# The causal attention product moved from the second slot of a step to the end of the first

## The reference, cut to what matters

```python
xn = layernorm(x)
# causal attention, 16 heads of 16
score = einsum('bhqd,bhkd->bhqk', Q, K) / sqrt(16) + mask
a = einsum('bhqk,bhkd->bhqd', softmax(score), V) @ WO
# attention with experts, 16 heads of 64, 8 experts, the best 2 of them
gv, go = gate(x, Wsel_v), gate(x, Wsel_o)
v   = einsum('bsd,bhse,hedp->bhsp', x, gv, Wv)
att = softmax(einsum('bhsp,bhtp->bhst', rope(x Wq), rope(x Wk)) / sqrt(64))
o   = einsum('bhst,bhtp->bhsp', att, v)
src = layernorm(x + einsum('bhsp,bhse,hepd->bsd', o, go, Wo))
y   = layernorm(src + relu(src @ W1 + b1) @ W2 + b2)
out = x + a + y
```

## Time and profile before

| what | value |
|---|---|
| time, median of 3 executions | 3246.9 us (3245.41 to 3250.37) |
| the profiled execution's own time | 3245.74 us |
| its span, first to last instruction | 3243.9 us |
| mean granted clock of TensorE | 0.991 of full speed |
| TensorE busy with matmuls | 3145.1 us, 97% |
| VectorE busy | 2480.0 us, 76% |
| ScalarE busy | 2017.9 us, 62% |
| GpSimd busy | 1477.1 us, 46% |

### The profile page before, as it was taken

The page is one execution under the profiler, slowest core; times in us unless marked ns, Lnnn a source line. Parts: engine busy times, 40 slices in busy tenths (PEclk is TensorE's granted clock), DMA queues, the critical chain, the costliest instruction groups (busy, mean ns, idle before and its releaser), DMA issues.

```text
span 3243.9 us, 67075 instructions
## 1 busy us (share of the span) xinstructions
PE 3145.1 (97%) x19648; PEld 2408.8 (74%) x19648; DVE 2480.0 (76%) x4686; ACT 2017.9 (62%) x4635; POOL 1477.1 (46%) x1231
## 2 busy tenths in 40 slices
PE   4899999999999999999999999999999999998997
PEld 3677777777777777777777777777777777775886
DVE  7777777777777778777787777777777777776896
ACT  4666666666666666666666666666666666664443
POOL 5233544335543444334543444434444543446677
PEclk8999999999999999999999999999999999999999
DMA  5232332333333332333323333243332433324222
GB/s 189 79 92 72 106 98 75 85 96 101 79 80 85 96 101 73 86 101 90 91 72 88 94 96 90 70 109 85 88 86 74 109 85 88 80 73 119 79 85 78
DMA packets 116202, 294.25 MB, mean 91 GB/s; under 512 B 33856, under 2 KB 54592, under 8 KB 99776
## 3 DMA queue, kind: packets, MB, share of 16 engines
q1 hardware_dynamic: 116160, 293.73, 33.9%
HBM read 261.69 MB, written 31.98 MB: 91 GB/s over the span
## 4 chain that ended last, share of the span: by engine, by line
PE 89%; DVE 7%; ACT 1%; POOL 1%; issue 1%; DMA 0%; SPq 0%; DVEq 0%; POOLq 0%; ACTq 0%
PE bank L753 32%; PE bank L896 22%; PE bank L811 11%; PE bank L768 7%; PE bank L869 6%; PE bank L773 2%; PE bank L881 2%; PE bank L1005 2%; PE bank L849 2%; PE bank L840 2%; PE bank L774 1%; PE bank L1016 1%; DVE nmax L1344 0%; DVE root L1262 0%; DVE rstd L1264 0%
## 5 line engine op out<-in xcount | busy, mean ns | idle before, releaser
L609 POOL TENSOR_TENSOR u_l<-uf,u_h 128x512 fp32r<-128x512 f32 x508 | 671.1, 1332 | 1624.3 <-ACT u_h L1177 1624.3
L753 PE MATMUL bank<-wv_h,xx 128*128 128x512 f32 x2048 | 735.7, 410 | 5.2 <-DVE vm L1362 5.2
L1087 ACT ACTIVATE probs<-bank,nmax 128x512 f32<-128x512 f32 (+3 forms) x1024 | 591.4, 606 | 234.2 <-DVE nmax L1344 229.9
L1344 DVE TENSOR_REDUCE nmax<-bank 128x1 f32<-128x512 f32 (+3 forms) x1024 | 554.2, 583 | 80.3 <-PE bank L774 52.8
L753 PEld LDWEIGHTS bank<-wv_h,xx 128*128 128x128 f32 x2048 | 386.9, 189 | 168.6 <-issue 80.4
L1177 ACT ACTIVATE u_h<-uf 128x512 fp32r<-128x512 f32 x508 | 304.9, 627 | 314.0 <-DVE uf L1449 314.0
L811 PEld LDWEIGHTS bank<-ident_sb,probs 128*128 128x128 f32 x3328 | 388.3, 141 | 106.9 <-issue 52.9
L811 PE MATMUL bank<-ident_sb,probs 128*128 128x128 f32 x3328 | 450.7, 274 | 0.9 <-ACT stackT L1162 0.9
L896 PE MATMUL bank<-u_h,wo_h 128*128 128x512 f32 x1016 | 430.3, 423 | 7.7 <-ACT q_h L1177 6.2
L1362 DVE TENSOR_TENSOR vm<-bank,gv 128x512 f32<-128x512 f32 x512 | 351.2, 686 | 81.6 <-PE bank L753 81.6
L896 PE MATMUL bank<-u_l,wo_h 128*128 128x512 f32 x1016 | 404.6, 398 | 0.0
(11 more groups left out here) (201 smaller groups left out, 5468.3 us busy)
## 6 DMA issues: line engine op xcount, KB each, us to landing
go<-go_d SPq DMA_DIRECT2D x256, 512.0 KB, 6.5
xx<-xs_d SPq DMA_DIRECT2D x126, 512.0 KB, 3.3
oo<-scale_d SPq DMA_DIRECT2D x128, 128.0 KB, 2.9
a_d<-a_out SPq DMA_DIRECT2D x128, 128.0 KB, 2.3
st<-in_wv SPq DMA_DIRECT2D x16, 512.0 KB, 5.6
st<-in_wo SPq DMA_DIRECT2D x16, 512.0 KB, 7.9
pt_c<-in_x SPq DMA_DIRECT2D x12, 512.0 KB, 4.8
go_d<-go_turned SPq DMA_DIRECT2D x256, 8.0 KB
```

What stands on the lines that cost most here:

```text
L609: nc.gpsimd.tensor_tensor(low, full, high.bitcast(f32), ALU.subtract).then_inc(ul_done, 1)
L753: last = nc.tensor.matmul(out, lhs, rhs, start=n == 1, stop=n == 3 * len(chunks))
L1087: nc.scalar.activation(probs[:, s % 2, j, 0:w], sbank[j][:, 0:w], ACT.Exp, bias=nmax[:, 2 * s + j:2 * s + j + 1], **kw).then_inc(exp_done, 1)
L1344: nc.vector.tensor_reduce(nmax[:, 2 * s + j:2 * s + j + 1], sbank[j][:, 0:w], AX.X, ALU.max, negate=True).then_inc(nmax_ready, 1)
```

## The change

In the table of TensorE's jobs, `AC` moves from the head of slot 1 to the end of slot 0. In an INNER step TensorE issued the scores of unit 1, `P` 0 to 3, `AT`, the transposes of unit 0, the scores of unit 2, `AC`, `V` 0, `V` 1. It now issues the scores of unit 1, `P` 0 to 3, `AT`, `AC`, the transposes of unit 0, the scores of unit 2, `V` 0, `V` 1. The tables of the other engines stay as they are. `AC` stays the sixth of the jobs that share the two banks, so the banks and the semaphore counts are the same.

```diff
-PE_FILL = [[("P", 0), ("P", 1), ("P", 2), ("P", 3), ("AT", 0)],
-           [("AC", 0), ("V", 0), ("V", 1), ("J", 0)],
+PE_FILL = [[("P", 0), ("P", 1), ("P", 2), ("P", 3), ("AT", 0), ("AC", 0)],
+           [("V", 0), ("V", 1), ("J", 0)],
            [("J", 1)],
            [("V", 2), ("J", 2), ("J", 3)],
```

## The result

| | before | after |
|---|---|---|
| median | 3247.1 us (3245.41 to 3251.13, 6 runs) | 3263.1 us (3261.7 to 3265.54, 6 runs) |
| span of the profiled execution | 3243.9 us | 3261.6 us |
| granted clock of TensorE, mean | 0.991 | 0.992 |

The ratio is 1.0049, with a 95% interval of 1.0038 to 1.0061: slower by half a per cent, 16 us. The forecast was 3264.

What follows compares the result with a forecast made beforehand. TensorE's issue time plus its few stalls was taken to bound the kernel. 55 usual steps × 0.33 us, less 0.7 in the seven late ones, made +17.5 us on 3245.7: 3263.2, as median 3264; range 3246 to 3287.

Steps and rivals of the forecast that it cites:

- The change of form: TensorE, AT and AC touching in 32-column pieces: V 0 comes 0.13 to 0.14 us earlier, 8.5 us over 63 steps.
- The maximum of unit 2: VectorE's row maximum, a sign: waits for TensorE's line 768 every step, starting 6.66 us behind AT, 0.92 late.
- ScalarE's copy stops waiting: Sign: the copy of a_out no longer waits for TensorE, so GpSimd's UL 1 starts about 7.3 us behind AT.
- Lines 1387, 1388 and 1390 are held: VectorE's CH 1, stretched by GpSimd instead of line 1404; U 2 comes 0.55 us late, the step grows by 0.33.
- The stall: TensorE's scores of unit 4 wait 0.46 us for the exponential of unit 3 in nearly every step.
- LAST: The step without CH 1 and P: up to 1 us either way, taken as 0.
- The late steps: 7 of 62 INNER steps whose maximum of unit 2 is already late: 0 to −0.2 us each, together −0.7.
- 0.92 us of lateness less 0.37 us from GpSimd's being out of the way sooner: VectorE, from the maximum of unit 2 to U 2: the two give U 2 0.55 us late.
- only the change of form counts: Rival: CH 1 slips through between GpSimd's instructions, unit 4 doesn't stall; 3238 us, faster; chance 0.12.

Runs made afterwards that it cites:

- third experiment: Changed kernel with RP 0 on GpSimd moved behind UL 2 and UL 3; 3234.1 us, ratio 0.9960.
- first experiment: Kernel before, TensorE's program untouched, with UH 1 ahead of the copy of AC on ScalarE; 3258.6 us, ratio 1.0033.
- the rope edit: RP 0 on GpSimd moved behind UL 2 and UL 3; on the changed kernel 3234.1 us, on the kernel before 3243.1 us.
- the second: Changed kernel with the scores of unit 2 issued ahead of the transposes of unit 0, directly behind AC; 3250.0 us, ratio 1.0010.

## Why the prediction was right, point by point

- *The change of form saves 0.13 to 0.14 us a step.* Right: 0.14 from `AT` to `V` 0, and 7.9 us, where the forecast had 8.5, between two kernels without the stall.
- *The maximum of unit 2 starts 6.66 us behind `AT`, after a wait.* Right to 0.01, with a wait of 0.84.
- *ScalarE's copy stops waiting, and `UL` 1 starts about 7.3 us behind `AT`.* Right: it starts at 7.28. ScalarE's queue had been standing behind a wait for TensorE, and the change took the wait away.
- *Lines 1387, 1388 and 1390 are held, `U` 2 is 0.55 us late, the scores of unit 4 start at 14.27 behind `AT`, 0.33 us a step.* Measured: 0.55, 14.26, 0.32. The stall was put at 0.46 us: the list shows a wait of 0.39, and the scores start 0.46 later than in the third experiment, where they don't wait (13.80). The time followed: +17.7 us of span against 17.5. LAST, taken as nothing within 1 us, gained 1.14, and that was made up outside the steps; the last few tenths of the agreement are luck.
- *The late steps gain 0 to 0.2 us each.* Off by little: three gained 0.08, four lost 0.09. `UL` 1 and line 1387 start there within 0.02 us of each other: where line 1387 is held (1.43 us) `U` 2 starts at 13.24, where `UL` 1 is (1.44 us) at 13.07 or 13.09.
- *"0.92 us of lateness less 0.37 us from GpSimd's being out of the way sooner."* The sum was right; as a reading of two causes it doesn't hold, as the two don't add. The traces have all four combinations:

| maximum of unit 2, us behind `AT` | `UL` 1 | `U` 2 | where |
|---|---|---|---|
| 5.74 | 8.42 | 11.81 | before, usual steps |
| 5.74 | 7.20 | 12.28 | first experiment, usual steps |
| 6.66 | 7.28 | 12.36 | changed kernel, usual steps |
| 6.65 | 8.42 | 13.18 | before, late steps |

With the maximum on time, GpSimd's coming sooner is no relief: it costs 0.47 us. With the maximum late it is one, of 0.8 us, and with GpSimd sooner the late maximum costs only 0.08 more. What counts is which instructions of `CH` 1 the three of GpSimd meet. In the first row only line 1404 is held for long, as the rope instructions fall mostly beside line 1405, which reads one tensor and takes 0.95 us in every trace. In the other rows three two-input lines are held, and the end of the second rope instruction sets `U` 2. With the rope instructions away, the late maximum and the sooner `UL` 1 together cost nothing (13.80). The last row comes from other steps, in which more is late than the maximum; no run makes the maximum alone late in a usual step.

- Of the rivals, "only the change of form counts" names what is left when the hold is gone: forecast 3238, measured 3234 with the rope edit, 4.7 us of which that edit gives by itself. It asked for `CH` 1 to slip through between GpSimd's instructions, and those were in the way.

## What to carry to other kernels

When a job moves on one engine, follow what it releases as much as what it delays: a copy that had been waiting runs sooner, and whatever stands behind it in that queue runs sooner too, perhaps straight into a third engine's critical stretch. Where a narrow chain passes through two-input VectorE instructions, look what GpSimd does at that time, and move GpSimd's deferrable work first; reordering VectorE's own list twice only moved the stall to the next buffer. A move that removes a cost of the bounding engine shows its gain only when the slack that it uses up is given back somewhere.

## What the runs showed of the hardware

- A VectorE instruction with two SBUF inputs that starts while a GpSimd one runs does its whole work behind it. One of 0.29 us (128x128) ends 0.15 us behind GpSimd's end, whatever is left of GpSimd's when it starts: it took 1.40 us in the first experiment, 0.54 in the changed kernel. `U` 3, 0.68 us of work (128x512), ended 0.55 behind `UL` 2 where `V` 0 stood ahead of it (1569.17 against 1568.62). In both it is the instruction's own time less 0.13 to 0.14. The reductions between them are not held (0.29 throughout), nor is line 1362, whose other input is in PSUM (0.68 us).
- A one-input instruction can be held too: line 1396, a TENSOR_SCALAR of 0.23 us, took 1.48 us in the late step shown and ended 0.08 behind GpSimd; it is held so in each of the seven.
- The hold works in both directions: where VectorE's started 0.03 us ahead of it, GpSimd's `UL` 1 took 1.41 us and not 1.29. The Trainium skill, SBUF — State Buffer, section Who interferes with whom, says that the issue order decides who blocks; the trace agrees: in the first experiment `UL` 1 started 0.05 us ahead of line 1387 and VectorE lost 1.1 us, in the second 0.03 behind it and GpSimd lost 0.13.
- On TensorE, from `AT` to `V` 0, the same products in four orders: with four changes of form (before, and `AC` between transposes and scores) `V` 0 starts 6.70 us behind `AT`, with three (the changed kernel) 6.56, with two (scores of unit 2 behind `AC`) 6.39. Each change of form less saved 0.14 to 0.17 us.
